# Deeper rings for raw expert weights, an earlier start of their loads, and another way to read a token list

## The reference

```python
gu = ragged_dot(xs, swapaxes(gate_up_proj, 1, 2), group_sizes)
gate, up = split(gu, 2, axis=-1)
hact = silu(gate) * up
y = ragged_dot(hact, swapaxes(down_proj, 1, 2), group_sizes)
out = zeros_like(x).at[tok].add(y * w[:, None])
```

## Time and profile before

| | us |
|---|---|
| median of three timed runs | 804.4 (804.34 to 804.52) |
| the profiled execution's own time | 807.05 |
| its span in the profile | 805.3 |
| plan known, first weight load issued | 179.4 |
| first list load issued | 198.94 |
| first gate product | 214.58 |
| merge of the two sums issued | 773.3 |

### The profile page before, as it was taken

One profiled execution on the slowest core, in us unless ns is written; L12 is line 12 of the kernel. 1 busy time (PEld: TensorE's weight loads), 2 busy tenths in 40 slices (PEclk: granted clock), 3 DMA queues, 4 the chain that ended last, 5 costly groups with the idle time before them and its releaser, 6 DMA issues. The chain is left out here.

```text
span 805.3 us, 15215 instructions
## 1 busy us (share of the span) xinstructions
PE 676.6 (84%) x4278; PEld 560.5 (70%) x4278; DVE 541.6 (67%) x1213; ACT 450.7 (56%) x891; POOL 516.2 (64%) x461
## 2 busy tenths in 40 slices
PE   4999999630599999999998998999988998989730
PEld 2555565320589999888988888878877977878630
DVE  5699898861276667776677777776767777767611
ACT  3444454310366666666775766757666676666610
POOL 6037777776738877887766666676657666666421
PEclk9999999855599999999999999999999999999965
DMA  8999999505659999999999999999999999999576
GB/s 304 349 313 332 322 330 301 170 12 159 177 154 220 244 240 237 239 247 255 247 268 256 268 241 259 245 245 258 236 260 217 250 236 245 233 246 232 107 132 152
DMA packets 107557, 189.93 MB, mean 236 GB/s; under 512 B 33521, under 2 KB 35441, under 8 KB 106065
## 3 DMA queue, kind: packets, MB, share of 16 engines
q1 hardware_dynamic: 74274, 125.61, 50.2%
q0 software_dynamic: 33200, 63.35, 38.9%
HBM read 143.40 MB, written 56.24 MB: 248 GB/s over the span
## 5 line engine op out<-in xcount | busy, mean ns | idle before, releaser
L1223 PE MATMUL bank<-xh,w1h 128*128 128x256 f32 (+7 forms) x768 | 229.3, 299 | 21.4 <-DVE h L887 21.2
L1224 PE MATMUL bank<-xl,w1h 128*128 128x256 f32 (+7 forms) x768 | 220.5, 287 | 0.0
L1225 PE MATMUL bank<-xh,w1l 128*128 128x256 f32 (+7 forms) x768 | 220.4, 287 | 0.0
L608 POOL DMA_INDIRECT xg<-normed_tokens,list x145 | 159.3, 1099 | 62.5 <-issue 55.9
L1223 PEld LDWEIGHTS bank<-xh,w1h 128*128 128x128 f32 x768 | 147.5, 192 | 27.0 <-issue 26.7
L617 POOL DMA_INDIRECT out_rows<-ys,list x73 | 116.7, 1599 | 72.9 <-ACT ys L1040 60.4
L903 DVE TENSOR_TENSOR xl<-bank,xh 128x448 fp32r<-128x448 f32 (+3 forms) x145 | 84.3, 616 | 115.1 <-ACT xh L1047 115.0
L592 POOL DMA_INDIRECT list_table<-token,slot x112 | 112.4, 1004 | 69.7 <-ACT token L1001 35.9
L617 POOL DMA_INDIRECT second_sum<-ys,list x70 | 111.2, 1589 | 64.5 <-ACT ys L1040 43.5
L1224 PEld LDWEIGHTS bank<-xl,w1h 128*128 128x128 f32 x768 | 147.9, 193 | 0.1
L1225 PEld LDWEIGHTS bank<-xh,w1l 128*128 128x128 f32 x768 | 147.6, 192 | 0.0
(11 more groups left out here) (204 smaller groups left out, 1084.7 us busy)
## 6 DMA issues: line engine op xcount, KB each, us to landing
raw<-in_w SPq DMA_DIRECT2D x195, 256.0 KB, 4.7
raw<-in_w2a SPq DMA_DIRECT2D x65, 256.0 KB, 5.0
ctxT_s<-in_ctxT SPq DMA_DIRECT2D x16, 768.0 KB, 7.3
ctx_s<-in_ctx SPq DMA_DIRECT2D x16, 768.0 KB, 8.8
raw<-in_w2b SPq DMA_DIRECT2D x65, 128.0 KB, 5.9
list_table<-blank SPq DMA_DIRECT2D x30, 256.0 KB, 7.6
x_in<-in_x SPq DMA_DIRECT2D x16, 224.0 KB, 4.5
out_rows<-x SPq DMA_DIRECT2D x16, 224.0 KB, 8.8
```

The costliest lines, as they stand in the source:

```text
L608: pool.indirect_dma_start(xg[u.on(XGS)][0:u.m, t, :], None, normed, bass.IndirectOffsetOnAxis(ap=lists[u.on(LISTS)][0:u.m, t, 0:1], axis=0 ...
L1223: pe.matmul(bank[m][:, 0:W], wh, mh, start=(c == 0), stop=False)
L1224: pe.matmul(bank[m][:, 0:W], wh, ml, start=False, stop=False)
L1225: mm = pe.matmul(bank[m][:, 0:W], wl, mh, start=False, stop=(c == DK - 1))
```

## The change

Four things. The ring of raw w1 buffers grows from three to six, that of raw w2 from two to five; the added buffers are allocated at the end, in the room that the first stage has left. SP loads w1 of units 0 to 4 and w2 of units 0 to 3 before it waits for the entries, and w1 of 5 and w2 of 4 after the first four lists. In the loop the weight loads run five and four units ahead of r instead of two and one. And a list's entries `p * nt` to `p * nt + nt - 1` go side by side to partition `p`, so that entry `p * nt + t` belongs to tile `t`.

```diff
--- before.py
+++ after.py
@@ -67,7 +67,7 @@
 TILES_BEFORE = [sum(nt for nt, m in RANKED[:u]) for u in range(STATIC + 1)]
 SUM_TILES = [sum(nt for nt, m in RANKED[i::2]) for i in range(2)]
 WIDE = max(nt * m for nt, m in RANKED)
-RAW1, LISTS, XGS = 3, 8, 3
+RAW1, RAW2, FRONT, LISTS, XGS = 6, 5, 5, 8, 3
 W1_PARTS = 3
 W1_PART = DK * 2 * F // W1_PARTS
 XS, CTXS, STORED = 6, 3, 3
@@ -220,7 +220,7 @@
         prow = sb("prow", [1, 2 * E + 2 * MAX_OVER + 1], I32)
 
 
-        raw1 = [sb(f"raw1_{i}", [P, DK * 2 * F]) for i in range(RAW1)]
+        raw1 = [sb(f"raw1_{i}", [P, DK * 2 * F]) for i in range(3)]
         raw2 = two("raw2_", [P, 2, D])
         w1h = [sb("w1h0", [P, DK, 2 * F], F32R)]
         w1l = [sb("w1l0", [P, DK, 2 * F], F32R)]
@@ -271,6 +271,8 @@
         hh = two("hh", [P, 2, WIDE], F32R)
         hl = two("hl", [P, 2, WIDE], F32R)
         ys = two("ys", [P, 3, D])
+        raw1 += [sb(f"raw1_{i}", [P, DK * 2 * F]) for i in range(3, RAW1)]
+        raw2 += [sb(f"raw2_{i}", [P, 2, D]) for i in range(2, RAW2)]
 
 
         const_pool = sem("const_pool"); const_dve = sem("const_dve"); const_in = sem("const_in")
@@ -286,7 +288,7 @@
         exps_sb = sem("exps_sb"); rough_s = sem("rough_s")
         tabled = [sem(f"tabled{i}") for i in range(4)]
         plan_ps = sem("plan_ps"); c_plan = sem("c_plan")
-        w1_in = [sem(f"w1_in{i}") for i in range(RAW1)]; w2_in = sem2("w2_in")
+        w1_in = [sem(f"w1_in{i}") for i in range(RAW1)]; w2_in = sems("w2_in", RAW2)
         list_in = [sem(f"list_in{i}") for i in range(LISTS)]
         gathered = [[sem(f"gathered{i}_{t}") for t in range(3)] for i in range(XGS)]; scattered = sem2("scattered"); cleared_sum = sem("cleared_sum"); merged = sem("merged"); kept = sem("kept")
         w1h_s = sem("w1h_s"); w1l_s = sem("w1l_s"); w2h_s = sem("w2h_s"); w2l_s = sem("w2l_s")
@@ -473,7 +475,7 @@
                 else:
                     i = bass.ds(u.n - STATIC + 2 * E, 1) if u.loop else slice(2 * E, 2 * E + 1)
                     at = sp.value_load(prow[0:1, i], min_val=0, max_val=PAD_LIST)
-                rows = table[bass.ds(at, u.rows), :].rearrange("(t p) c -> p t c", p=u.m)
+                rows = table[bass.ds(at, u.rows), :].rearrange("(p t) c -> p t c", p=u.m)
                 sp.dma_start(lists[u.on(LISTS)][0:u.m, 0:u.nt, :], rows).then_inc(list_in[u.on(LISTS)], 16)
 
             def load_w1(u):
@@ -485,27 +487,32 @@
                                  ).then_inc(w1_in[u.on(RAW1)], 16)
 
             def load_w2(u):
-                split_wait(sp, w2l_s, u.units_freed(2))
+                split_wait(sp, w2l_s, u.units_freed(RAW2))
                 e = weights_of(u)
-                sp.dma_start(raw2[u.on(2)][:, 0, :], w2a[bass.ds(e, 1)].rearrange("a p f -> (a p) f")).then_inc(w2_in[u.on(2)], 16)
-                sp.dma_start(raw2[u.on(2)][0:FR, 1, :], w2b[bass.ds(e, 1)].rearrange("a p f -> (a p) f")).then_inc(w2_in[u.on(2)], 16)
+                sp.dma_start(raw2[u.on(RAW2)][:, 0, :], w2a[bass.ds(e, 1)].rearrange("a p f -> (a p) f")).then_inc(w2_in[u.on(RAW2)], 16)
+                sp.dma_start(raw2[u.on(RAW2)][0:FR, 1, :], w2b[bass.ds(e, 1)].rearrange("a p f -> (a p) f")).then_inc(w2_in[u.on(RAW2)], 16)
 
             load_w1(Unit(0))
             load_w1(Unit(1))
             load_w2(Unit(0))
-            load_w1(Unit(2))
-            load_w2(Unit(1))
+            for n in range(2, FRONT):
+                load_w1(Unit(n))
+                load_w2(Unit(n - 1))
             for i in range(4):
                 sp.wait_ge(tabled[i], B // 4 * ENTERS * 16)
             for n in range(4):
                 load_list(Unit(n))
+            for n in range(FRONT, RAW1):
+                load_w1(Unit(n))
+            for n in range(FRONT - 1, RAW2):
+                load_w2(Unit(n))
             for r in range(STATIC):
-                if r + 4 == STATIC:
+                if r + RAW1 == STATIC:
                     sp.wait_ge(c_plan, PLAN)
                 early_stage(load_list, r + 4)
                 if r > 0:
-                    early_stage(load_w1, r + 2)
-                early_stage(load_w2, r + 1) if r > 0 else None
+                    early_stage(load_w1, r + RAW1 - 1)
+                    early_stage(load_w2, r + RAW2 - 1)
 
             def next_over(u):
                 load_list(u)
@@ -519,7 +526,7 @@
             sp.wait_ge(merged, 16)
             split_wait(sp, list_in[LAST.on(LISTS)], (overs + LAST.turn(LISTS) + 1) * 16)
             split_wait(sp, w1_in[LAST.on(RAW1)], (overs + LAST.turn(RAW1) + 1) * 16 * W1_PARTS)
-            split_wait(sp, w2_in[LAST.on(2)], (overs + LAST.turn(2) + 1) * 32)
+            split_wait(sp, w2_in[LAST.on(RAW2)], (overs + LAST.turn(RAW2) + 1) * 32)
             split_wait(sp, gathered[LAST.on(XGS)][0], (overs + LAST.turn_of_tile(XGS, 0) + 1) * 16)
 
 
@@ -913,8 +920,8 @@
                 dve.wait_ge(w2h_s, u.n + 1)
                 wait(dve, y_ps, u.tiles_freed(2))
                 b = u.on(2)
-                v.tensor_tensor(w2l[b][:], raw2[b][:, 0, :], w2h[b][:, 0, :].bitcast(F32), ALU.subtract)
-                v.tensor_tensor(w2h[b][FR:P, 1, :], raw2[b][0:FR, 1, :], w2h[b][0:FR, 1, :].bitcast(F32),
+                v.tensor_tensor(w2l[b][:], raw2[u.on(RAW2)][:, 0, :], w2h[b][:, 0, :].bitcast(F32), ALU.subtract)
+                v.tensor_tensor(w2h[b][FR:P, 1, :], raw2[u.on(RAW2)][0:FR, 1, :], w2h[b][0:FR, 1, :].bitcast(F32),
                                 ALU.subtract).then_inc(w2l_s, 1)
 
             w1_low(Unit(0))
@@ -1052,11 +1059,11 @@
                 a.copy(w1h[u.on(2)][:].rearrange("p c f -> p (c f)"), raw1[u.on(RAW1)][:]).then_inc(w1h_s, 1)
 
             def w2_high(u):
-                act.wait_ge(w2_in[u.on(2)], (u.turn(2) + 1) * 32)
+                act.wait_ge(w2_in[u.on(RAW2)], (u.turn(RAW2) + 1) * 32)
                 wait(act, y_ps, u.tiles_freed(2))
                 b = u.on(2)
-                a.copy(w2h[b][:, 0, :], raw2[b][:, 0, :])
-                a.copy(w2h[b][0:FR, 1, :], raw2[b][0:FR, 1, :]).then_inc(w2h_s, 1)
+                a.copy(w2h[b][:, 0, :], raw2[u.on(RAW2)][:, 0, :])
+                a.copy(w2h[b][0:FR, 1, :], raw2[u.on(RAW2)][0:FR, 1, :]).then_inc(w2h_s, 1)
 
             w1_high(Unit(0))
             x_high(Unit(0), (0, 1, 2))
```

## The result

| | before | changed |
|---|---|---|
| median of 20 timed runs (us) | 804.64 (803.59 to 807.6) | 807.5 (806.05 to 809.4) |
| ratio | | 1.0032, 95% interval 1.0024 to 1.004 |
| span of the profiled execution | 805.3 | 806.1 |

The changed kernel is slower by 0.32%, 1.9 to 3.2 us by the interval. The spans differ by 0.8 us only: the profiled execution of before took 807.05 us, 2.4 more than the median of its kernel, that of the changed kernel 807.91, 0.4 more. What follows are the places of the profile after that answer to the rows of before. The page first: TensorE's share is 83% instead of 84%, and the small packets are fewer by 8,865, from 33,521.

A forecast was written before the change was run, and what follows sets the result against it. TensorE alone was taken to set the pace from 226 to 400 us; later its wait for `h` was an engine loop, the seam hanging on entries, first list, gathers. +0.9 - 0.2 + 0.6 - 1.0 = +0.3 us gave 804.7 us, range 798.0 to 807.5.

The forecast's parts named there:

- likeliest case: Whole kernel: nothing that is waited for moves by much more than 1 us; 803.0 to 806.4 us, chance 0.58.
- collision rival: Seam between the stages: prefetch takes DMA engines while entries, first list and gathers are the path; 808.8 us, chance 0.19.
- Its sign: Seam: the collision rival decides once the first gate product starts later than 216.5 us.
- the other signs: Profile after: first list 198.9 to 200.8, `h` waits 18.3 within 2, gather waits 6.5 to 9.5 us, packets about 8,800 fewer.
- Ring depths in the steady state: Steady units: each SP step is released at the same moment and moves the same bytes; 0 us.
- Four more loads ahead of the lists: Seam: the last entry DMA now flies beside full queues and lands later; +0.9 us (0 to +1.9).
- SP itself isn't late: Seam: two more pairs of loads end at 196.7 us, 2.2 us before the first list.
- Lists at the seam: Seam: lists read side by side need 128 packets instead of 384; -0.2 us (0 to -0.8).
- Two loads between lists 3 and 4: Seam: 1.18 MB more fly beside the five gathers TensorE waits for, priced at the fifth; +0.6 us (0 to +1.5).
- Lists in the steady state: Steady units: fewer list packets shorten TensorE's waits for gathers, ten times 0.1 us; -1.0 us (+1.0 to -8.5).
- rival of relieved DMAs: Units: if 64 B packets cost far more among full queues, the gathers' 8.5 us of waits go; 797.2 us, chance 0.23.
- three seam terms: Seam: +0.9 for four loads ahead of the lists, -0.2 for side-by-side lists, +0.6 for two loads between lists.

The follow-up runs named there:

- lists alone: The kernel before with one line changed, a list's entries side by side per partition: 804.23 us, ratio 0.9987.
- rings alone: The changed kernel with the list line of before, on two other chips: 848.79 against 839.94 us (ratio 1.0107), again 849.31 against 840.64 (1.0097).

## Why the prediction was right and where it was not

The forecast was 804.7 us with a range of 798.0 to 807.5; 807.5 was measured, its upper edge: that it still lies inside is luck. The likeliest case (0.58) had 803.0 to 806.4 and nothing that moves by much more than 1 us; the kernel became 0.32% slower, and in time and mechanism this is nearest to the collision rival (0.19, 808.8 us), whose entries and gathers both came out late. Its sign, a first gate product later than 216.5 us, did not show as read (215.65), but with the last entry as late as before it would have been 216.54. Of the other signs, the first list (198.99), `h` (17.7 us) and the packets (8,865 fewer) came as said; the waits for gathers (11.3) left their 6.5 to 9.5.

- *Ring depths in the steady state, 0*: right. The 61 units took the same time within 0.04 us, and no new wait for `raw` appeared (ACT's one wait at the start was 5.6 us instead of 6.4).
- *Four more loads ahead of the lists, +0.9*: right in size, 0.94 us measured. "SP itself isn't late" was right for this chip, by a margin of 2.2 us that I had worked out and not looked at further (4.6 us in the profile, where the plan was known 2.6 us earlier). On the chips where the entries end before SP's issue, the same loads cost 8.2 us. The rule of the Trainium skill ("DMA: Bandwidth & Descriptors", section on queues, rings and completion order), that an engine takes turns between queue rows, agrees in kind with entries that land in 1.97, 2.91 and 3.46 us as the weights come nearer.
- *Lists at the seam, -0.2*: -0.04 us measured in the change, and -0.12 to -0.15 in the three other kernels with the new layout against before, so the sum's term was a little too large. The Trainium skill ("DMA: Bandwidth & Descriptors", section on the anatomy of one DMA, written for DMAs that GpSimd issues) would make it 0, as many descriptors are said to come before their cost shows: nearer in the changed kernel, not in the three others.
- *Two loads between lists 3 and 4, +0.6*: mis-sized, 1.06 us measured from first gather to gate product (within its 0 to +1.5), and at another tile. I priced the fifth gather; the second was hit (2.7 us late), because it is issued 1 us behind w1 of unit 5.
- *Lists in the steady state, -1.0*: the step that failed. "Where TensorE waits for a gather, that much comes off" holds only if nothing else ends later in the loop. The waits for gathers were 11.3 us instead of 8.5 and the units took the same time, 529.75 us against 529.79; lists alone and three more kernels show the same with waits from 8.2 to 13.2 us. In place of -1.0 the runs show 0. TensorE has slack in these units and next meets the wait for `h`. As far as the chain of the earlier trace rows shows, the loop of DVE and ACT ends later; I had read it and still added up TensorE's stalls. By the same runs the rival of relieved DMAs had nothing to win: its 8.5 us were not on the path.
- *The sum*: with the steady term at 0 and the three seam terms as measured, +2.0 us; the steps of the two profiles show +1.7, the medians +2.9 (+2.6 by the ratio). A rest of about 1 us is not explained. It could be in the first stage; no run shows it.

## What to carry to other kernels

A wait seen on the busiest engine is worth something only if the unit's period moves with it: compare periods between like units before pricing a stall. The total of such waits also varies between profiles by itself (here from 8.2 to 13.2 us), so a change in it is no finding yet. Filling idle DMA time is free only while the small transfer that releases the next stage is not among it, and while the queue that issues it has nothing in front of that transfer; a margin of 2 to 5 us there is a matter of which chip one gets. Where a ring has slack, try to hold the prefetch back until the first gathers have landed, rather than issue it as early as possible: it gained 1.7 us on one chip and, with the new lists, nothing on two others.

## What was not expected of the hardware

- Chips differ: the same program took 805.0 us on one and 839.9 and 840.6 us on two others, mainly in the first stage. The order in which entries and weight issue end was the other way round there, and a change that cost 0.3% on one (rings and lists) cost 1.0% on the others (rings alone).
- The landing of a 64 B scatter of 128 entries grew from 1.97 to 3.46 us as the last weight load moved from 7.7 to 0.2 us before its issue.
- 3.5 MB of weights between lists 3 and 4, 2.4 of them issued beside the first gathers, delayed the first gate product by 1.4 us, 1.2 MB by 1.1 us.
- The longest stall alone doesn't tell whether the clock falls: it stayed at 1.00 after one of 1.42 us, averaged 0.58 over 4 us after one of 2.44 us at the same place, and 0.57 after two of 1.09 and 0.90 us.
- TensorE's clock fell to 0.88 over 10 us in the middle of the experts and no unit took longer.
- On two chips ACT's first silu started up to 3.3 us after its input was done, on the third within 0.04 us, and no trace says why.
